# A mixture of 32 experts by sorted nodes, and edge transfers split in two

## The reference

```python
def _L1_ffn_ref(x, router_w, router_b, W1, b1, W2, b2):
    ...
    logits = xf @ router_w.T + router_b
    idx = jnp.argmax(logits, axis=-1)
    w1t = jnp.take(W1, idx, axis=0)             # 256 x 64 each
    h = jnp.einsum('nd,ndh->nh', xf, w1t) + jnp.take(b1, idx, axis=0)
    h = jax.nn.relu(h)
    w2t = jnp.take(W2, idx, axis=0)             # 64 x 256 each
    out = jnp.einsum('nh,nhd->nd', h, w2t) + jnp.take(b2, idx, axis=0)
    out = jax.nn.relu(out)
```

## Time and profile before

| | us |
|---|---|
| median of 3 runs | 7885.76 (7880.52 to 7893.24) |
| the profiled execution | 7827.13 |
| its span in the trace | 7825.4 |
| PE busy | 5375.0 |
| DVE busy | 4168.1 |
| POOL busy | 3553.2 |
| ACT busy | 2370.7 |

### The profile page before, as it was taken

One profiled execution on the slowest core, in us unless ns is written; L12 is line 12 of the kernel. 1 busy time (PEld: TensorE's weight loads), 2 busy tenths in 40 slices (PEclk: granted clock), 3 DMA queues, 4 the chain that ended last, 5 costly groups with the idle time before them and its releaser, 6 DMA issues. The chain is left out here.

```text
span 7825.4 us, 86636 instructions
## 1 busy us (share of the span) xinstructions
PE 5375.0 (69%) x22652; PEld 3704.3 (47%) x22653; DVE 4168.1 (53%) x11843; ACT 2370.7 (30%) x4657; POOL 3553.2 (45%) x3101
## 2 busy tenths in 40 slices
PE   2886477777639866769797667639995454554585
PEld 1554356566526644446454455525663333332374
DVE  9102488888853367764455677782224344333544
ACT  1222344444302223322112555542331221121132
POOL 4777677777560257750001454500005772776043
PEclk9999677777759988889798677768997767666687
DMA  2444333333230265550001222200003332333323
GB/s 53 118 118 95 92 112 111 108 110 110 75 95 30 49 126 163 159 142 1 8 10 33 68 71 67 69 6 13 13 8 89 93 88 59 91 91 87 95 81 102
DMA packets 392190, 607.94 MB, mean 78 GB/s; under 512 B 158638, under 2 KB 276444, under 8 KB 390890
## 3 DMA queue, kind: packets, MB, share of 16 engines
q0 software_dynamic: 174592, 350.59, 17.4%
q1 hardware_dynamic: 216990, 247.74, 11.0%
q10 hardware_dynamic: 308, 6.40, 0.3%
HBM read 458.94 MB, written 144.63 MB: 77 GB/s over the span
## 5 line engine op out<-in xcount | busy, mean ns | idle before, releaser
L779 POOL DMA_INDIRECT conv_rows<-rows_b,index x832 | 849.6, 1021 | 1286.8 <-SPq L2560 949.7
L811 DVE TENSOR_TENSOR acc<-acc,ps 125x257 f32 (+1 forms) x1664 | 701.6, 422 | 952.1 <-DMA mpnn_edge<-records_src 325.9
L2606 PE MATMUL ps<-conv_rows,conv_weight_of 128*125 128x256 f32 x1664 | 619.4, 514 | 620.1 <-issue 292.7
L332 POOL DMA_INDIRECT records_src<-by_src_edge_stage,by_src_edge_slot x400 | 562.5, 1406 | 498.7 <-DMA by_src_edge_stage<-edge_rows 378.6
L2606 PEld LDWEIGHTS ps<-conv_rows,conv_weight_of 128*125 128x125 f32 x1664 | 365.4, 246 | 874.1 <-issue 559.3
L779 POOL DMA_INDIRECT mpnn_rows<-rows_b,index x416 | 480.0, 1154 | 321.4 <-POOLq L1615 124.1
L496 POOL DMA_INDIRECT records_dst<-front_back,front_dst_addr x400 | 503.2, 1258 | 260.2 <-issue 260.2
L779 POOL DMA_INDIRECT gat_rows<-rows,index x416 | 500.9, 1204 | 259.5 <-PE ps L1089 138.7
L779 POOL DMA_INDIRECT hyp_rows<-rows,index x416 | 416.6, 1002 | 407.8 <-PE ps L2208 273.9
L1417 PE MATMUL ps<-room,experts_w 128*128 128x500 f32 (+1 forms) x1344 | 547.8, 545 | 64.8 <-DMA experts_w<-in_L_ffn_w 40.2
L1576 ACT ACTIVATE experts_hid<-ps,experts_consts 128x500 f32<-128x500 f32 (+1 forms) x448 | 302.4, 678 | 937.3 <-PE ps L1417 830.4
(11 more groups left out here) (572 smaller groups left out, 10616.1 us busy)
## 6 DMA issues: line engine op xcount, KB each, us to landing
mpnn_edge<-records_src SPq DMA_DIRECT2D x104, 512.0 KB
edge_rows<-front_edge_ring SPq DMA_DIRECT2D x100, 503.9 KB
by_src_edge_stage<-edge_rows SPq DMA_DIRECT2D x100, 503.9 KB
conv_rows<-rows_b,index POOLq DMA_INDIRECT x832
front_attr<-in_edge_attr SPq DMA_DIRECT2D x100, 125.0 KB
rows_b<-acc SPq DMA_DIRECT2D x15, 560.0 KB
second_w<-in_L_ffn_w SPq DMA_DIRECT2D x1, 8192.0 KB
gat_rows<-rows,index POOLq DMA_INDIRECT x416
```

What stands on the lines that cost most here:

```text
L332: pool.indirect_dma_start(out=self.S.records["src"], out_offset=bass.IndirectOffsetOnAxis(ap=self.addr[:, c:c + 1], axis=0), in_=self.stag ...
L779: pool.indirect_dma_start(out=rows[:, n % U, t, :], out_offset=None, in_=table, in_offset=bass.IndirectOffsetOnAxis(ap=ends[:, n * G + t:n ...
L811: dve.tensor_tensor(here, here, S.ps[0:P, t % banks, 0:width], ALU.add).then_inc(added, 1)
L2606: pe.matmul(S.ps[0:P, t, 0:D], weight_of[:, q.slot, t, :], rows[:, q.slot, t, :], start=True, stop=True).then_inc(summed, 1)
```

## The change

1. The second mixture goes by sorted nodes. `expert_weights` only picks; SP stores the normalised rows to `rows_b` and loads both weights, with the second bias as row 65 of the second weights (`w2[F1:F1 + 1]`), and the first bias. `sort_picks`, now with sizes as arguments, sorts the nodes over 32 experts into 56 tiles of 128 slots. `one_expert_each` (new) puts each tile through its one expert and stores the results in the order of slots; POOL then gathers them, block by block, and DVE adds them to the residual and takes the statistics of layer norm 4, which no longer takes its own.
2. In `sort_picks` the chain of compares that gives each tile its expert is one compare and one sum.
3. `ffn3` has 64 tiles instead of 68.
4. Four transfers of 125 partitions (the attributes' loads, the stores of the edges' rows, and the stage loads of `EdgeScatter`) become two each, of 13 and of 112 partitions (`move_rows`, with `SPLIT` 112), and their waits count 32 instead of 16.

```diff
--- before.py
+++ after.py
...
-            sp.dma_start(self.stage[:, r], view[:, k * SG:(k + 1) * SG, :]).then_inc(self.loaded[r], 16)
+            move_rows(sp, self.stage[:, r], view[:, k * SG:(k + 1) * SG, :], self.loaded[r])
...
-                pool.wait_ge(self.loaded[r], 16 * (k // self.RING + 1))
+                pool.wait_ge(self.loaded[r], ROWS_IN * (k // self.RING + 1))
...
-                        sp.dma_start(attr[:, g % AR], attributes[:, (g + AR) * AG:(g + AR + 1) * AG, :])\
-                            .then_inc(attr_in[g % AR], 16)
+                        move_rows(sp, attr[:, g % AR], attributes[:, (g + AR) * AG:(g + AR + 1) * AG, :],
+                                  attr_in[g % AR])
                     sp.wait_ge(edge_out, 3 * (g + 1))
-                    sp.dma_start(out[:, g * AG:(g + 1) * AG, :], ring[:, g % ER]).then_inc(rows_stored[g % ER], 16)
+                    move_rows(sp, out[:, g * AG:(g + 1) * AG, :], ring[:, g % ER], rows_stored[g % ER])
...
+NE1 = 32
+F1 = 64
+NODE_TILES = (N + NE1 * 127) // 128
+assert NODE_TILES % U == 0
+def one_expert_each(nc, S, expert_of, node_of, slot_of, w1, b1, w2, weights_in, rows_out):
+    T, RR = NODE_TILES, 6
+    with phase(nc, "mlp1") as (sb, sem):
+        rows = sb("rows", [128, RR, D])
+        rows_t, aside = sb("rows_t", [128, U, K, 128]), sb("aside", [128, 2, K, F1])
+        hid, bias, y = sb("hid", [F1 + 1, 2, 128]), sb("bias", [F1, U]), sb("y", [128, U, D])
+        gathered, stored = [sem(f"gathered{u}") for u in range(RR)], [sem(f"stored{u}") for u in range(U)]
+        results = [sem(f"results{c}") for c in range(NB // LEAD)]
+        ones, turned, turned_out, set_aside, bias_in, first, hidden, second, evacuated, joined = (
+            sem(x) for x in ("ones", "turned", "turned_out", "set_aside", "bias_in", "first", "hidden", "second",
+                             "evacuated", "joined"))
+        def experts_of(eng, n):
+            _, values = nc.values_load_multi_w_load_instructions(
+                expert_of[0:1, n:n + U], engines=[eng.engine], min_val=0, max_val=NE1 - 1,
+                skip_runtime_bounds_check_because="the sort of the picks counts the starts of experts 1 to NE1 - 1 "
+                                                  "that lie at or below the tile")
+            return values
+        with nc.Block() as block:
+            @block.sync
+            def _(sp):
+                for m in range(T):
+                    sp.wait_ge(evacuated, m + 1)
+                    sp.dma_start(S.slots[m * 128:(m + 1) * 128, :], y[:, m % U, :]).then_inc(stored[m % U], 16)
+            @block.gpsimd
+            def _(pool):
+                pool.wait_ge(rows_out, ROWS_IN)
+                for n in range(T):
+                    if n >= RR:
+                        pool.wait_ge(turned, n - RR + 1)
+                    pool.indirect_dma_start(
+                        out=rows[:, n % RR, :], out_offset=None, in_=S.rows_b,
+                        in_offset=bass.IndirectOffsetOnAxis(ap=node_of[:, n:n + 1], axis=0))\
+                        .then_inc(gathered[n % RR], 16)
+                for u in range(U):
+                    pool.wait_ge(stored[u], T // U * 16)
+                for t in range(NB):
+                    pool.indirect_dma_start(
+                        out=S.acc[:, t, 0:D], out_offset=None, in_=S.slots,
+                        in_offset=bass.IndirectOffsetOnAxis(ap=slot_of[:, t:t + 1], axis=0))\
+                        .then_inc(results[t // LEAD], 16)
+            @block.tensor
+            def _(pe):
+                chosen = {}
+                pe.wait_ge(weights_in, 64)
+                pe.wait_ge(ones, 1)
+                for n in range(T + 2):
+                    if n % U == 1 and n < T:
+                        chosen[n // U] = experts_of(pe, n - 1)
+                    if n < T:
+                        pe.wait_ge(gathered[n % RR], (n // RR + 1) * 16)
+                        if n >= 2:
+                            pe.wait_ge(turned_out, n - 1)
+                        for k in range(K):
+                            ins = pe.transpose(S.ps[:, n % 2, k * 128:(k + 1) * 128],
+                                               rows[:, n % RR, k * 128:(k + 1) * 128], S.ident[:])
+                        ins.then_inc(turned, 1)
+                    m = n - 1
+                    if 0 <= m < T:
+                        pe.wait_ge(turned_out, m + 1)
+                        pe.wait_ge(set_aside, m + 1)
+                        if m >= 2:
+                            pe.wait_ge(hidden, m - 1)
+                        for k in range(K):
+                            ins = pe.matmul(S.ps[0:F1, 2 + m % 2, 0:128], aside[:, m % 2, k, :], rows_t[:, m % U, k, :],
+                                            start=k == 0, stop=k == K - 1)
+                        ins.then_inc(first, 1)
+                    m = n - 2
+                    if m >= 0:
+                        e = chosen[m // U][m % U]
+                        pe.wait_ge(hidden, m + 1)
+                        if m >= 2:
+                            pe.wait_ge(evacuated, m - 1)
+                        pe.matmul(S.ps[:, 4 + m % 2, 0:D], hid[:, m % 2, :],
+                                  w2[:, bass.ds(e, 1), :].rearrange("p a d -> p (a d)"),
+                                  start=True, stop=True).then_inc(second, 1)
+            @block.scalar
+            def _(act):
+                for n in range(T + 1):
+                    if n < T:
+                        act.wait_ge(turned, n + 1)
+                        act.copy(rows_t[:, n % U],
+                                 S.ps[:, n % 2, 0:K * 128].rearrange("p (k n) -> p k n", k=K)).then_inc(turned_out, 1)
+                    m = n - 1
+                    if m >= 0:
+                        act.wait_ge(bias_in, m + 1)
+                        act.wait_ge(first, m + 1)
+                        if m >= 2:
+                            act.wait_ge(second, m - 1)
+                        act.activation(hid[0:F1, m % 2, :], S.ps[0:F1, 2 + m % 2, 0:128], ACT.Relu,
+                                       bias=bias[:, m % U:m % U + 1]).then_inc(hidden, 1)
+            @block.vector
+            def _(dve):
+                dve.memset(hid[F1:F1 + 1], 1.0).then_inc(ones, 1)
+                dve.wait_ge(weights_in, 64)
+                for n in range(T + 2):
+                    if n < T:
+                        if n % U == 0:
+                            chosen = experts_of(dve, n)
+                        if n >= 2:
+                            dve.wait_ge(first, n - 1)
+                        e = chosen[n % U]
+                        dve.tensor_copy(aside[:, n % 2], w1[:, bass.ds(e, 1)].rearrange("p a k f -> p (a k) f"))\
+                           .then_inc(set_aside, 1)
+                        if n >= U:
+                            dve.wait_ge(hidden, n - U + 1)
+                        dve.tensor_copy(bias[:, n % U:n % U + 1], b1[:, bass.ds(e, 1)]).then_inc(bias_in, 1)
+                    m = n - 2
+                    if m >= 0:
+                        dve.wait_ge(second, m + 1)
+                        if m >= U:
+                            dve.wait_ge(stored[m % U], m // U * 16)
+                        dve.tensor_copy(y[:, m % U, :], S.ps[:, 4 + m % 2, 0:D]).then_inc(evacuated, 1)
+                for t in range(NB):
+                    if t % LEAD == 0:
+                        dve.wait_ge(results[t // LEAD], LEAD * 16)
+                    dve.scalar_tensor_tensor(S.x[:, t, :], S.acc[:, t, 0:D], 0.0, S.x[:, t, :], ALU.max, ALU.add)\
+                       .then_inc(joined, 1)
+                    for old in (t - 3,) if t < NB - 1 else range(t - 3, NB):
+                        if old >= 0:
+                            dve.wait_ge(joined, old + 1)
+                            dve.bn_stats(S.acc[:, old, D:D + 6], S.x[:, old, :])
...
-PICK_TILES = (2 * N + NE3 * 127) // 128 + 1
-PICK_TILES += -PICK_TILES % U
...
+PICK_TILES = (2 * N + NE3 * 127) // 128
+assert PICK_TILES % U == 0
...
+def sort_picks(nc, S, NE, PC, T, C, key, expert_of, node_of, begin, pick_of=None, slot_of=None, scratch=None):
...
+                if slot_of is not None:
+                    ch.step(dve.tensor_copy(slot_of, pos[:]))
...
-                ch.link(dve.tensor_scalar(blk[0:1], iota_t[0:1], start[0:1, 1:2], None, ALU.is_ge))
-                for e in range(2, NE3):
-                    ch.link(dve.scalar_tensor_tensor(blk[0:1], iota_t[0:1], start[0:1, e:e + 1], blk[0:1],
-                                                     ALU.is_ge, ALU.add))
-                ch.step(dve.tensor_copy(expert_of[:], blk[0:1, :]))
+                ch.link(dve.tensor_tensor(begun[:], bc(iota_t[0:1], NE - 1), bc_mid(start[0:1, 1:NE], T), ALU.is_ge))
+                ch.link(dve.tensor_reduce(blk[:], begun[:], AX, ALU.add))
...
+                if pick_of is None:
```

(20 more changed lines are left out.)

107 lines of the change are left out of this document (44 added, 63 removed).

## The result

The changed kernel takes 7594.6 us (median of 4 runs, 7591.72 to 7612.88); the kernel before, beside it, 7883.14 (7871.01 to 7893.24). The ratio is 0.9639, 95% interval 0.9619 to 0.9660: 288.5 us less. The forecast was 7530 with a range of 7462 to 7592, so the direction was right, the gain was 64.6 us smaller than forecast, and the time lies just outside the range.

The account below looks back on a forecast made before the run. No engine is full overall; the kernel is a row of stages, each with its own bound. -301 - 18 - 26 - 10 = -355 takes the profiled 7827.13 to 7472; keeping 58.6 to the median gives 7530, range 7462 to 7592.

Parts of the forecast that it names:

- (c): Second mixture's tiles: a gather each 1.26 us sets the pace, TensorE just behind at 1.1; 56 tiles take 70.6 us.
- rival A: Second mixture's tiles run at half clock, 2.3 us each, 129 instead of 70.6: +58, 7590; chance 0.08.
- the forecast's -301: Second mixture, router's product to layer norm 4's aggregate: 492.6 us before, 301 less after, bounds -309 and -275.
- Sort: Second mixture, between router and first gather: sorting nodes over 32 experts takes 32 us, bounds 28 and 37.
- rival E: Second mixture: SP's queue is held by many small pieces, PE waits for weights: +5 to +40, 7550; chance 0.08.
- Way back: Second mixture after the tiles: 25 gathers at 1.26, 31.5 us, then landing, last joins and statistics, barrier; aggregate at 3941.
- the 4 us for contention: Second mixture's way back: joins with two SBUF inputs slow GpSimd's gathers, 0 to 10 us, taken as 4.
- Last mixture: 64 tiles for 68 at 3.73 us gives -14.9, compares and smaller groups -3: -18, bounds -15 and -20.
- Split: Split transfers: shorter GpSimd stops at the front, -26; shorter waits for edges' loads, -10; the loop's 88 us not counted.
- every 43rd: Front loop: GpSimd stands at every 43rd scatter, eight times, mean 7.6 us from scatter to scatter.
- Rivals B and C: B: front loop's gain shows, another 50 to 60, 7475, chance 0.07; C: part 3's stops and waits stay, +36, 7566, 0.10.
- The profiled execution's distance to the median: Whole kernel: profiled execution, 7827.13, lies 58.6 us below the runs' median, 7885.76; the forecast keeps this distance.

Follow-up runs that it names:

- the changed kernel's second trace: The changed kernel with no edit, run again on one of the chips with 7490 us: ratio 0.9600 to the kernel before.

## Why the forecast was wrong, point by point

**The second mixture, wrong.** The step that failed is (c), "the gather sets the pace, PE just behind: 56 x 1.26". It took TensorE's time per record from the last mixture at full clock. TensorE set the pace instead, at 2.62 us a tile. Two things were off. The granted clock was 0.50, rival A, which had 0.08: the argument against it, that the last mixture comes out of the same sort and has 0.99, compared what lies ahead of the tiles and not what is in them. The traces show that the work inside matters: with 128 columns of weights in the first layer, or an extra full-width matmul, the clock is 1.00 in nearly all of the tiles; with a matmul as long on 32 columns it is 0.50. What lies ahead matters too: behind 24 warming matmuls the same thin tiles held 1.00. And a tile costs TensorE 1.43 at full clock and 2.62 at half, against the forecast's 1.1 and rival A's 2.3: with 64-column weights between full-width ones each record of 128 columns took some 0.15 us instead of 0.11, and each of the second layer's 0.27 instead of 0.22. An estimate from these steps for 56 tiles: 1.43 for 1.26 costs 10 us, and 2.62 for 1.43 another 67, so the clock is the larger part. Together they made rival A's price 58 where it was 75, and the range ended just below the time. What stays open is why the same tiles are at the high clock in one execution and at the low one in the next.

With the weights widened and the reads spread the gathers are 1.25 apart and the stretch takes 210.1 us; the forecast's -301 means 208.4. So router, sort, way back and the rest of the sum stand, and so does the gather's pace once each tile's records cost what the forecast took for them.

**Sort.** Right: 32.9 us, 3785.87 to 3818.74, for 32. **Late weights**, rival E: nothing was late; TensorE began 3.0 us after the first gather, where 4.7 was forecast.

**Way back.** Right in the sum, 46.9 for 45, by two errors: the gathers are 1.51 apart instead of 1.26 from the first one on, which are ahead of any join, so that isn't VectorE's work beside them (what it is stays open); and the 4 us for contention didn't come. The Trainium skill's rule on shared interfaces ("GPSIMD Engine Reference", "Specifications") would have stretched the 25 gathers beside the joins; this trace doesn't show it: all but two of the 24 steps are 1.51 to 1.54, with and without a join beside them, and the two are 1.57 and 1.66.

**Last mixture.** Right, 17.3 for 18, and 15.6 of them are the four tiles.

**Split.** Right in size and in place: -29 at the front (forecast -26), -8 to -10 at the first mixture (-10), the loop 87 us faster and hidden (88). The stops take 3.9 us from scatter to scatter where the forecast had 3.6. The prediction's count of them, eight, was right, and its "every 43rd" was not: they are 39 scatters apart, which changes nothing in the sum. Rivals B and C fall.

**The profiled execution's distance to the median.** The forecast kept 58.6 us between them; after the change the profiled execution lies 0.8 above the median. That cost nothing, since the medians fell by about what the touched stages gave. As far as two executions can tell, the first profiled one was short in the attention, the message network and the hyperbolic layer: these add +59 after the change with the same computation there, and the sum of the four touched stages, -283.6, is what the medians show, -288.5.

**The clock.** In the changed kernel's second trace TensorE was busy 140.00 us of 140.00 in the second mixture's tiles and stayed at 0.50. The Trainium skill ("TensorE: Matmul & The Clock Gate", "What's actually happening") ties the release of the clock to how busy TensorE has been. This trace disagrees, if busy means busy time.

## What to carry to other kernels

Sorting to one expert pays even with this: 226 of 509 us gone, and 299 with two small edits. But when an edit makes the weights of matmuls narrower, price TensorE at both clocks, and look at the granted clock inside the new stretch first; filling idle columns with zeros can be the cheapest way to get the clock back (here 65 us for a memset and a wider copy's target). Padding that nobody uses still reads: let it read different rows.

## What the runs showed of the hardware

- TensorE's clock had two resting points under thin work: tiles with 64-column weights held 1.00 for 42 tiles once they had it, and 0.50 for 33 tiles after a pause of 10.9 us, with TensorE without idle time in both. In the three traces of the changed kernel the clock was 0.50 in two and rose for 6.9 us in one. Of its twelve executions one was about 60 us shorter.
- With 128-column weights it came back within 7 us each time that it fell among the tiles (seven times in five of the seven traces, after 3.4 to 6.8 us). With an extra 256-column matmul on 128 columns of weights it rose and stayed; with one on 32 columns of weights it stayed at 0.50, though one execution in four had the time of the high clock.
- At full clock a record of a product with 128 moving columns took 0.11 us where all first-layer weights were 128 columns wide (tile 1.10) and about 0.15 where 64-column weights stood between full-width ones (tile 1.43).
- Gathers of 128 rows that are all the same row took the mean step of a tile from 1.27 to 2.05 us, at a DMA share of 0.94 for 133 GB/s, against 0.67 for 201 GB/s with different rows. At half clock, with a gather only every 2.62 us, their pieces of 4 KB took 0.3 us and not 0.75, and they held nothing up.
- Open: the common pauses of about 2 us of all engines on the slower chips, and why the stages with gathers differ by 3 to 11% between chips.
